# Linear attention on Trainium2: the context folded into the output weights before the queries meet it

## The reference, cut to what matters

```python
def linear_attn(q, k, v):
    scale = DH ** (-0.25)
    q = jax.nn.softmax(q * scale, axis=-1)
    k = jax.nn.softmax(k * scale, axis=-2)
    context = jnp.einsum('bhnd,bhne->bhde', k, v)
    return jnp.einsum('bhnd,bhde->bhne', q, context)
...
h = layer_norm(x, ln1_g, ln1_b)
...
x = x + attn @ wo + bo
h = layer_norm(x, ln2_g, ln2_b)
x = x + jax.nn.gelu(h @ w_ff1 + b_ff1) @ w_ff2 + b_ff2
```

## Time and profile before

| | us |
|---|---|
| median of 3 executions | 1536.88 |
| the three executions | 1536.88, 1543.87, 1535.32 |
| the profiled execution, its own time | 1545.4 |
| its span, first to last instruction | 1543.6 |
| time outside the span | 1.8 |
| mean granted TensorE clock | 0.975 |

### The profile page before, as it was taken

How to read it: one execution, slowest core, us unless ns; L and a number is a source line. 1 busy time by engine, 2 the same in 40 slices (tenths; PEclk the granted TensorE clock), 3 DMA queues, 4 the chain that set the end, 5 groups by cost and what they waited for, 6 DMA issues and landing times. The chain is left out here.

```text
span 1543.6 us, 19029 instructions
## 1 busy us (share of the span) xinstructions
PE 1452.9 (94%) x6910; PEld 848.3 (55%) x6914; DVE 986.8 (64%) x1506; ACT 753.1 (49%) x1237; POOL 494.0 (32%) x410
## 2 busy tenths in 40 slices
PE   6999999989999999888999998898889999999998
PEld 3757764432232265453444443322568888888886
DVE  5774243768877743548888783676677575664853
ACT  5466344443334451543666565434655545445442
POOL 0046420123132410343111112102136655655562
PEclk9999997999999999998999999899999999999999
DMA  7000000000000000083535300000313223223201
GB/s 293 1 0 0 1 1 4 0 1 1 0 1 1 1 0 0 1 164 42 125 51 74 42 3 1 4 1 4 133 42 110 69 83 100 78 74 104 73 10 55
DMA packets 39044, 67.55 MB, mean 44 GB/s; under 512 B 3944, under 2 KB 19368, under 8 KB 38568
## 3 DMA queue, kind: packets, MB, share of 16 engines
q1 hardware_dynamic: 38952, 66.33, 16.1%
HBM read 57.80 MB, written 8.39 MB: 43 GB/s over the span
## 5 line engine op out<-in xcount | busy, mean ns | idle before, releaser
L2255 ACT ACTIVATE arena<-psum 128x512 f32<-128x512 f32 (+1 forms) x304 | 155.2, 583 | 109.9 <-PE psum L2100 109.2
L2303 DVE TENSOR_REDUCE b_mx<-psum 128x1 f32<-128x512 f32 (+3 forms) x304 | 179.6, 650 | 45.0 <-PE psum L2078 36.9
L3047 POOL TENSOR_TENSOR m_w_rest<-m_w,m_w_high 128x512 fp32r<-128x512 f32 (+1 forms) x88 | 111.6, 1270 | 155.6 <-ACT m_w_high L3246 155.6
L3497 DVE TENSOR_TENSOR m_hidden<-m_gelu,psum 128x512 f32<-128x512 f32 (+1 forms) x88 | 60.4, 686 | 148.6 <-ACT m_gelu L3338 124.4
L3140 PE MATMUL psum<-m_x_high,m_w_high 128*128 128x512 f32 (+1 forms) x352 | 138.4, 393 | 3.2 <-issue 3.2
L3053 POOL TENSOR_TENSOR m_h_rest<-m_hidden,m_h_high 128x512 fp32r<-128x512 f32 (+1 forms) x88 | 122.4, 1390 | 58.9 <-ACT m_h_high L3260 58.9
L3140 PE MATMUL psum<-m_x_rest,m_w_high 128*128 128x512 f32 (+1 forms) x352 | 138.0, 392 | 0.0
L3140 PE MATMUL psum<-m_x_high,m_w_rest 128*128 128x512 f32 (+1 forms) x352 | 138.0, 392 | 0.0
L3338 ACT ACTIVATE m_gelu<-psum 128x512 f32<-128x512 f32 (+1 forms) x88 | 52.5, 596 | 120.7 <-PE psum L3140 120.6
L1998 POOL TENSOR_SCALAR_AFFINE_SELECT arena<-arena 128x512 f32<-128x512 f32 x64 | 40.1, 637 | 212.7 <-ACT arena L2255 212.7
L1359 ACT ACTIVATE x_probs<-psum 128x1024 f32<-128x1024 f32 x56 | 57.3, 1024 | 90.9 <-PE psum L1097 90.9
(11 more groups left out here) (591 smaller groups left out, 3238.6 us busy)
## 6 DMA issues: line engine op xcount, KB each, us to landing
m_w<-w SPq DMA_DIRECT2D x32, 512.0 KB, 4.6
m_wo<-wo SPq DMA_DIRECT2D x16, 512.0 KB, 4.0
weights_sb<-weights SPq DMA_DIRECT2D x2, 2820.0 KB, 12.2
m_w<-w SPq DMA_DIRECT2D x16, 344.0 KB, 4.7
b_q_stack<-b_q_dram SPq DMA_DIRECT2D x36, 128.0 KB, 5.9
b_k_stack<-b_k_dram SPq DMA_DIRECT2D x36, 128.0 KB, 6.0
weights_sb<-weights SPq DMA_DIRECT2D x1, 3328.0 KB, 14.0
b_q_dram<-b_q_parts SPq DMA_DIRECT2D x6, 512.0 KB, 3.4
```

The lines of the kernel that those rows point to most:

```text
L2255: act.activation(quad_of(g)[:, heads[0]:heads[-1] + 1, 0:n], score(i)[:, 0:len(heads) * n].rearrange("p (h n) -> p h n", n=n), ACT.Exp, sc ...
L2303: dve.tensor_reduce(mx[:, part, qi, heads[0]:heads[0] + nh], tile(("piece", p))[:, 0:nh * keys].rearrange("p (h n) -> p h n", n=keys), AX, ...
L3047: pool.tensor_tensor(w_rest[:, n % W_RING, :, :, 0:H_N(n % HT)], raw_of(n), w_high[:, n % W_RING, :, :, 0:H_N(n % HT)].bitcast(F32), ALU.s ...
L3497: dve.tensor_tensor(hidden[rows, n % 2, :], gelu[rows, n % 2, :], c.bank(2 + n % 2)[rows, :], ALU.mult)\
```

## The change

Instead of multiplying the queries by the context and the result by the output weights, the kernel first multiplies the context by the output weights (the fold, 256 x 256 per sequence) and then the queries by the fold.

- `attend` on PE and `copy_attended` on ACT are gone for both sequences.
- `fold_context(b)` on PE multiplies the transposed context by `a_wo`: two matmuls of 128x256 into bank 1. The operands of `contexts` are swapped so that the context comes out transposed.
- `copy_context` on DVE copies the four diagonal blocks without scaling them. The inversion is a step of its own, `invert_keys`. `scale_fold(b)` on DVE multiplies the fold by the inverse on its way from PSUM to SBUF: two instructions of 128x256.
- `project` multiplies the fold by the turned queries, eight matmuls of 128x512 as before.
- In PE's order `fold_context(0)` stands between the second and the third piece of `queries(1)`, and `fold_context(1)` between the two halves of `variance(0)`. In DVE's order `scale_fold(0)` stands between the second and the third piece of `shift_queries(1)`. `invert_keys(1)` stands ahead of `normalise_queries(1)`, and `scale_fold(1)` follows `copy_context(1)`.

```diff
@@ PE
+                def fold_context(b):
                     pe.wait_ge(*sg[b]["ctx_copied"](1))
+                    pe.wait_ge(*sg[b]["q_copied"](2))
+                    for m in range(FT):
+                        mm = pe.matmul(bank(b, 1)[:, m * D:(m + 1) * D], context[:, b, m, :], c.w("a_wo", m, 0, D),
+                                       start=True, stop=True)
+                    mm.then_inc(sg[b]["folded"].sem)
+
+                def project(b):
+                    pe.wait_ge(*sg[b]["fold_copied"](1))
                     pe.wait_ge(*sg[b]["q_copied"](4))
                     for j in range(NCH):
                         for m in range(FT):
-                            pe.matmul(bank(b, 2 * j + m), context[:, b, m, :], qt[b][:, m, col(j)],
-                                      start=True, stop=True).then_inc(sg[b]["at_done"].sem)
-
-                def project(b):
-                    for j in range(NCH):
-                        pe.wait_ge(*sg[b]["at_copied"](2 * (j + 1)))
-                        for m in range(FT):
                             for k in range(FT):
-                                mm = pe.matmul(bank(b, 2 * j + m), c.w("a_wo", k, m * P, P), at[b][:, k, col(j)],
+                                mm = pe.matmul(bank(b, 2 * j + m), fold[b][:, k, m * P:(m + 1) * P], qt[b][:, k, col(j)],
                                                start=(k == 0), stop=(k == 1))
...
                 contexts(0)
-                queries(1)
-                attend(0)
+                queries(1, (0, 1))
+                fold_context(0)
+                queries(1, (2, 3))
                 turn_keys(1)
                 project(0)
                 turn_queries(1)
                 mean(0, ln2[0])
                 contexts(1)
-                variance(0, ln2[0])
-                attend(1)
+                variance(0, ln2[0], (0,))
+                fold_context(1)
+                variance(0, ln2[0], (1,))
                 project(1)
@@ ACT
                 exp_queries(1)
-                copy_attended(0)
                 copy_keys(1)
...
                 roots(0, ln2[0], c.eps)
-                copy_attended(1)
                 split_h2(0)
@@ DVE
+                def scale_fold(b):
                     dve.wait_ge(*sg[b]["k_step"](7))
-                    dve.wait_ge(zeroed, 1)
-                    dve.wait_ge(*sg[b]["ctx_done"](1))
+                    dve.wait_ge(*sg[b]["folded"](1))
                     for m in range(FT):
-                        for h in (0, DH):
-                            ins = dve.tensor_scalar(context[h:h + DH, b, m, h:h + DH], bank(b, 0)[h:h + DH, m * P + h:m * P + h + DH],
-                                                    k_r[h:h + DH, b, m:m + 1], None, ALU.mult)
-                    ins.then_inc(sg[b]["ctx_copied"].sem)
+                        ins = dve.tensor_scalar(fold[b][:, m, :], bank(b, 1)[:, m * D:(m + 1) * D], k_r[:, b, m:m + 1], None, ALU.mult)
+                    ins.then_inc(sg[b]["fold_copied"].sem)
...
                 normalise_once(1)
+                invert_keys(0)
                 copy_context(0)
-                shift_queries(1)
+                shift_queries(1, (0, 1))
+                scale_fold(0)
+                shift_queries(1, (2, 3))
+                invert_keys(1)
                 normalise_queries(1)
                 add_attended(0)
                 centre(0, ln2[0], of_y)
                 copy_context(1)
+                scale_fold(1)
                 normalise(0, ln2[0], "a_g2", "a_b2")
```

More of the change, by code:

```diff
@@ L203, in linear_attention_layer @@
             q_proj=4, q_step=12, q_shift=4, q_exp=4, q_norm=4, q_turned=4, q_copied=4,
-            ctx_done=1, ctx_copied=1, at_done=4, at_copied=4, o_done=4, y_done=4,
+            ctx_done=1, ctx_copied=1, folded=1, fold_copied=1, o_done=4, y_done=4,
             y2_done=4, d_done=4)) for b in range(B)]
@@ L231, in linear_attention_layer @@
         q_t = [room(b, 5).rearrange("p (u n) -> p u n", u=4) for b in range(B)]
-        at = [tiles(b, 5) for b in range(B)]
+        fold = [room(b, 5)[:, 0:FT * D].rearrange("p (m n) -> p m n", m=FT) for b in range(B)]
         y = h1
@@ L319, in folded_variance, with variance @@
                         pe.matmul(bank(b, 2 * j + 1), c.mean_w[:], squares[b][:, 0, col(j)], start=True, stop=True).then_inc(s["var"].sem)
-                def variance(b, s):
-                    for j in range(NCH):
+                def variance(b, s, js=range(NCH)):
+                    for j in js:
                         pe.wait_ge(*s["sq"](j + 1))
@@ L336, in keys, with by_token @@
                                     mm.then_inc(sg[b]["k_proj"].sem)
-                def by_token(b, name, free, done):
-                    for u in range(4):
+                def by_token(b, name, free, done, us=range(4)):
+                    for u in us:
                         pe.wait_ge(*free(u + 1))
@@ L348, in values, with queries @@
                     by_token(b, "a_wv", sg[b]["k_exp"], sg[b]["v_proj"])
-                def queries(b):
-                    by_token(b, "a_wq", sg[b]["v_copied"], sg[b]["q_proj"])
+                def queries(b, us=range(4)):
+                    by_token(b, "a_wq", sg[b]["v_copied"], sg[b]["q_proj"], us)
                 def turn_keys(b):
@@ L365, in contexts @@
                         for t in range(TT):
-                            mm = pe.matmul(bank(b, 0)[:, m * P:(m + 1) * P], ekt_t[b][:, t, m * P:(m + 1) * P],
-                                           v_t[b][:, t, m * P:(m + 1) * P], start=(t == 0), stop=(t == TT - 1))
+                            mm = pe.matmul(bank(b, 0)[:, m * P:(m + 1) * P], v_t[b][:, t, m * P:(m + 1) * P],
+                                           ekt_t[b][:, t, m * P:(m + 1) * P], start=(t == 0), stop=(t == TT - 1))
                     mm.then_inc(sg[b]["ctx_done"].sem)
@@ L378, in turn_queries @@
                         mm.then_inc(sg[b]["q_turned"].sem)
-                def attend(b):
+                def fold_context(b):
                     pe.wait_ge(*sg[b]["ctx_copied"](1))
+                    pe.wait_ge(*sg[b]["q_copied"](2))
[5 more added lines that the diff above has]
+                    pe.wait_ge(*sg[b]["fold_copied"](1))
                     pe.wait_ge(*sg[b]["q_copied"](4))
@@ L538, in copy_queries @@
                                        ACT.Copy).then_inc(sg[b]["q_copied"].sem)
[L540 to L544, removed]
                 def split_w(i):
@@ L660, in copy_values, with shift_queries @@
                            .then_inc(sg[b]["v_copied"].sem)
-                def shift_queries(b):
-                    for u in range(4):
+                def shift_queries(b, us=range(4)):
+                    for u in us:
                         dve.wait_ge(*sg[b]["q_proj"](u + 1))
@@ L680, in copy_context, with invert_keys @@
                 def copy_context(b):
+                    dve.wait_ge(zeroed, 1)
+                    dve.wait_ge(*sg[b]["ctx_done"](1))
+                    for m in range(FT):
+                        for h in (0, DH):
+                            ins = dve.tensor_copy(context[h:h + DH, b, m, h:h + DH], bank(b, 0)[h:h + DH, m * P + h:m * P + h + DH])
+                    ins.then_inc(sg[b]["ctx_copied"].sem)
+                def invert_keys(b):
                     dve.wait_ge(*sg[b]["k_exp"](4))
```

## The result

| | kernel before | changed kernel |
|---|---|---|
| median of 22 executions each | 1536.74 us | 1540.57 us |
| lowest to highest | 1534.79 to 1546.33 | 1537.87 to 1549.24 |
| profiled execution, its span | 1543.6 us | 1543.3 us |

The ratio is 1.0028, with a 95% interval of 1.0015 to 1.0041; it is not exactly that of the two medians, which is 1.0025. The change makes the kernel slower by a quarter of a per cent. That is less than the half per cent that the prediction called hard to tell, but the interval excludes 1. A second series, the changed kernel unaltered (11 executions against 33 of the kernel before on the same chip), gave 1.0023 (1.0014 to 1.0032).

The account below looks back on a forecast made before the run. PE's own work was taken to set most of the time, with a DVE, ACT and POOL chain binding here. 2.15 us (collision) + 0.86 (fold), rounded to 2.9, on the median 1536.88 gave 1539.8 us; range 1534 to 1547.5.

Parts of the forecast that it names:

- The likeliest case: Whole kernel: DVE and POOL collide as worked out, +2.9 us, 1539.8 us; chance 0.50.
- the short form of a rival: PE after 91.2 us: clock falls to 1.2 GHz, with the short loss of 1.8 us; the clock case had chance 0.16.
- PE's gain and where it stays: PE alone saves 6.0 us, but only 2.2 us, at project(0), is won before the next meeting with DVE.
- DVE's side of sequence 0: DVE around shift_queries(1): copy_context(0) stays 1.18 us; scale_fold(0) takes 0.85 us and fits without delay.
- The collision: DVE's normalisation and sums against POOL's subtractions: up to 2.4 us each time DVE is second; contexts(1) 2.15 us late.
- fold(1) in the chain: PE, inside variance(0): the fold moves the variance's end, and the roots hanging on it, by 0.86 us.
- The clock: PE between 91.2 and 97.4: clock may fall to 1.2 GHz; with the long loss +9.7 us, 1546.6 us; chance 0.16.
- the long loss: PE's clock after sparse work: 6.8 us given up in one stretch at 1.2 GHz, as at 240 to 280 us.
- The sum: Chain through sequence 1: 2.15 + 0.86 = +3.0 us, rounded to 2.9 for slack at the meeting of 118 us.
- PE's gain comes through: Rival, whole kernel: DVE's chain is no limit and PE's 6.0 us stand, 1530.9 us; chance 0.06.
- No collision: Rival, normalisation pieces 3 and 4 slip past POOL: chain 0.3 us late, 1537.2 us; chance 0.25.

Follow-up runs that it names:

- e4: Changed kernel with six unread 128x512 matmuls added on PE, around the second norm's means and before the feed-forward loop; 1540.04 us, ratio 1.0024.
- e2: Changed kernel with ACT's splits of three weight parts moved ahead of exp_queries(1); 1533.26 us, ratio 0.9983; once more 1535.84 us, ratio 0.9996.
- e7: Changed kernel with ACT's splits held until normalise_queries(1) is through; 1541.70 us, ratio 1.0031.
- e5: Changed kernel with ACT's splits ahead of exp_queries(1) and fold_context(1) after both halves of variance(0); 1534.40 us, ratio 0.9998.

## Why the prediction was right, point by point

The prediction was 1539.8 us, +2.9; measured were 1540.57 us, +3.8, and +3.6 in the second series. The likeliest case is the one that came, with the short form of a rival added. That the total comes so near is in part luck: the 1.8 us of the clock were not in the sum, the collision was 0.7 us too dear in it, and a median here is uncertain by one or two us.

- *PE's gain and where it stays.* The fold at 0.86 us, the stall at the fourth piece of turn_keys(1) (0.20 us), project(0) 2.2 us earlier (2.15) and the wait ahead of the loop, forecast at 2.5 us (2.38), are all in the trace. e4 and e2 show that PE's 6 us could not come through.
- *DVE's side of sequence 0.* scale_fold took 0.87 us for two (0.85 was worked out) and hid. The copy without scaling took 0.93 us instead of 1.18, which counts for nothing.
- *The collision.* Forecast were two L677 of up to 2.4 us more; they are 2.31 and 1.90 us long, 2.8 us more than undisturbed. The second L701, forecast 28.5 us after contexts(0) (96.5 - 68.03), ended at 27.80, 0.7 us sooner. The term that was mis-sized is POOL's run of three. I let it last from 84.7 to 93.1, 8.4 us; it started where forecast (16.6 us after contexts(0)) and lasted 7.9 us (83.31 to 91.19). e2 settles that the collision is the cause, and the stretch of e7 agrees.
- *fold(1) in the chain.* 0.86 us expected; e5 against e2 shows 0.86 us between contexts(1) and the variance's end. What reaches the end of the stretch is less (0.46), since another meeting with POOL takes part.
- *The clock.* The rival named the thin stretch between the turned queries and contexts(1), and the clock fell there. I had given this the long loss of 6.8 us or the short one of 1.8; it was about the short one: 0.91 us on the mean and 0.92 us on contexts(1), and e4 gave back 1.80 of it up to the variance and 1.46 in the stretch. The variance and project(1), which the rival let run slowly too, did not. This is what the forecast lacks. Its likeliest case ought to have carried at least the chance of it, because in the kernel before PE's pause of 2.45 us ahead of 230.80 stands where the earlier trace rows count 0.91, and the two waits that it worked out, 91.2 to 93.6 and from there to 96.5 less one mean, are about as long. It was not certain: behind a pause of 2.46 us in the same place, the second profile of the changed kernel has 1.00.
- *The sum.* At the end of the variance the chain was 4.29 us late (38.51 after contexts(0), before 34.22) where 3.0 were forecast: +0.92 for contexts(1) at the lower clock, and +0.36 for its later start, in which the mean's 1.87 us, forecast at 0.9, outweighs the 0.6 us by which the mean started sooner than forecast (27.85 us after contexts(0)). At the end of the stretch it was 4.07.
- *The other two rivals.* "PE's gain comes through" is excluded by e4. "No collision" is what e2 built, and there the stretch is 2.06 us below the kernel before where the rival had 0.3 above. The rival had left both L701 behind POOL, and e2 frees these as well, so the clock doesn't fall either.

The Trainium skill's rule in SBUF — State Buffer, section "SBUF: two separate sides", that two SBUF inputs on DVE and a reading GpSimd instruction exclude each other for a whole instruction, agrees with this trace: DVE's L672 of 2.31 us ended 0.54 us after POOL's subtraction, and POOL's pair took 5.58 us here against 4.67 in e2. DVE's instructions with one operand in PSUM were not held (L700, two in 1.40 us at 91.67, beside POOL's subtraction of 91.35 to 93.95).

What stays open: why the total varies by several us from one execution to the next. In the profiles, the code behind this part took between 1308.8 us (e2) and 1319.0 us (kernel before) with nothing changed in it. The granted clock differs there: between 230 and 400 us it is 0.93 in the kernel before, and in the two profiles of the changed kernel 0.94 (1315.9 us behind this part) and 0.99 (1309.3 us). The start of contexts(0) varied too, from 66.28 (e4) to 69.98 us (e7). I made no experiment on either.

## What to carry to other kernels

When work is taken off the engine that is busiest on average, look for the points where it waits for another chain: what is saved ahead of such a point is lost at it, and a step put into that chain lengthens it by its full length there (0.86 us here, of which 0.46 are left at the end of the stretch). An engine that loses work also starts its next steps earlier. Here ACT's earlier splits let POOL start while DVE still had two-input multiplications to do, and moving the splits to where ACT was idle and DVE read PSUM gave 6.1 us in the stretch, 2.1 us of them below the kernel before. For differences of one to four us in 1540, measure the stretch from a fixed row to a fixed row in the trace, and not the total alone.

## What the runs showed of the hardware that I had not expected

The stretch between two fixed rows repeated to 0.01 us in three pairs of profiles (154.56 and 154.56, 155.42 and 155.43, 153.32 and 153.33) and to 0.11 us in the pair where the clock fell, while the totals of one kernel in one series spread over 2.6 to 13 us.

The clock fell to 1.2 GHz after waits of PE of 0.48 and 2.11 us with 0.66 us of work between, and again after the 2.38 us ahead of the loop, but not after the 0.95 us at 94.28 in the kernel before, nor after the 0.45 us in e2. Nor does the wait alone decide: behind the pause of 2.45 us that follows this part, the clock from 220 to 240 us was 0.91 in the kernel before and 1.00 in the second profile of the changed kernel. In the two profiles of the changed kernel the same waits (2.11 and 2.10, 0.68 and 0.69 us) gave a contexts(1) of 4.49 and 4.64 us: the length of the slow stretch is not fixed by the program.
